# A fused decoder block on one core: setup and first two steps reordered, the second FFN matrix turned one step later, a table filled in the setup, gate sums ahead of the fourth up product

## Chip, cores, metric

One core of a Trainium2 chip runs the whole program. The metric is the device time of one execution in microseconds. The engines are TensorE (PE, matrix products), VectorE (DVE), ScalarE (ACT), GpSimd (POOL) and SyncE (SP, here the queue that issues every DMA).

## What is computed

The input x is 128 sequences of 128 tokens with 256 channels, and a context of the same shape. Three blocks with residuals follow one another:

```python
x = x + _L0_attn_ref(_layernorm(x), W_qkv, b_qkv, W_proj, b_proj)     # q k^T, a piecewise factor by bands, softmax, v, projection
x = x + _L0_xattn_ref(_layernorm(x), ctx_1024, ctx_1024, Wi_w, ...)   # 8 heads, gates and decay, normalised per head
x = x + _L0_ffn_ref(_layernorm(x), W1, b1, W2, b2, scale)             # 256 -> 1024 -> 256, gelu, a token-dependent low rank part
```

In the second block the decay between tokens i and j comes from running sums of log-sigmoid gates:

```python
itilde = einsum('bsd,hd->bhs', gate_in, Wi_w) + Wi_b
ftilde = einsum('bsd,hd->bhs', gate_in, Wf_w) + Wf_b
csum = cumsum(log_sigmoid(ftilde), axis=-1)
Dtilde = where(tril, csum_i - csum_j, -inf) + itilde_j
D = exp(Dtilde - max(Dtilde))
```

## The kernel before, in words

The 128 sequences are taken in 32 groups of four. A step `it` works on several groups at once, as a software pipeline: the first layernorm and the q and v products of group it+1 ("coming"), the self attention of group it ("own"), the gated attention of group it-1 ("cross"), and the FFN of group it-2 ("ffn"). Step 0 has the coming and own parts alone, step 1 has cross besides, and from step 2 on all four run. Steps 2 to 30 are a hardware loop, 31 to 33 are written out behind it.

There is no scheduler: each engine runs its own program in the order in which the code names the instructions, and waits on semaphore counters. What an engine waits for holds up everything behind it on that engine.

The **setup**. PE turns and multiplies the attention weights, DVE splits the results in a high and a low part, POOL writes constants. Each DVE instruction of it counts up the semaphore `s_set_v`. V_BIAS and SETUP_V are counts of it: after the biases, and after everything. `project(-1)` on PE (from L1259) makes q and v of the first group; before it PE waits for SETUP_V. POOL waits for V_BIAS, and adds the constant row `cvp` to `xb` (the residual of the attention; L610) in every step.

**W1 and W2** arrive as they lie in memory and have to be turned by PE. They are loaded into the space of `hs_all`, which the FFN first writes in step 2. `turn_w1` (L1349) writes four PSUM banks, ACT copies them to `W1h` (L746), DVE subtracts to `W1l` (L1091). `turn_w2(i)` (L1361), i from 0 to 3, writes a bank each, and ACT copies it to `W2f` (L834). In step 0, PE runs the scores (L1390), turn_w1, turn_w2(0) and (1), turns the softmax's probabilities (L1563), attends (L1574), turns xn1 (L1253), then turn_w2(2) and (3), and then `project(0)`. `turn_xn1` and the last two turns wait for ACT and for `x2` from DVE (L1147). `moving` (L1094) is a table of 32 heads by 128 columns, a sum of two small tables, which the decay products of the cross part use; DVE fills it in step 0 in two instructions. ACT's `apply_first` (L663) writes xn1, the normalised group to come.

**PE in a full step.** turn xn3 (L1253), scores (L1390), a product for the low rank part (L1409), turn xn2, then the eight up products `up(i)` (L1428) with other work between: up(0) into bank UA, `gates` (L1379), up(1) into UB, up(2) into PV, up(3) into TB, the first group of adapters `up_adapter(0)` (L1436), `sums` (L1385, L1386), up(4) into TA, `qk(0)` (L1453), up(5), up(6), qk(1), up(7), adapters again, then `decay` (L1528), `down` (L1490) and the rest. `sums` picks the gate's running sums out of `csum`. Behind it the chain on DVE is: copies of the two results to `acs` (L1042, L1043), a running maximum `acs` (L1045, semaphore acs_ok), then `em` (L1049), the split of the sums into `parts` (L1055 to L1059), and `rows` (L1063). The queue of SP copies `parts` into three rows of `moving` (L505). `qk` waits for acs_ok, since it writes the bank of `sums`:

```python
if t == 0:
    pe.wait_ge(h_ok.h, h_ok.at(it, 1))
    ...
    pe.wait_ge(acs_ok.h, acs_ok.at(it, 1))
    pe.wait_ge(gate_ok.h, gate_ok.at(it, 1))
```

`csum` itself is a scan on DVE (L1038) behind `gates`, two small DVE operations and three of ACT. POOL's order in a step is: ot (L594), vc (L600, L606), xb (L610), xg (L619, when the bands of the scores are done, y_ok), and four times Ng (L625).

Of the kernel before, what the change touches and what calls it, by code (L numbers as in the profile page):

```python
# [34 lines left out]
P = 128  # L35
D = 256
S = 128
G = 4
# [82 lines left out]
def build(nc, x, ctx_in, W_qkv, b_qkv, W_proj, b_proj, Wi_w, Wi_b, Wf_w, Wf_b, gn_w, gn_b,  # L121
# [10 lines left out]
    with ctx:  # L132
# [174 lines left out]
        RAWB = UAB + [PV, GT, DD, QQ] + UAB  # L307
# [220 lines left out]
        def _(pool):  # L528
# [60 lines left out]
            def step(it):  # L589
# [18 lines left out]
                if SELF.on(it):  # L608
                    pool.wait_ge(xb_loaded.h, xb_loaded.at(it, 16))
                    pool.tensor_tensor(xb[:, :, :], xb[:, :, :], cvp[:, :].unsqueeze(1).broadcast_to([P, G, D]),  # L610
                                       ALU.add).then_inc(xb_ok.h, 1)
# [21 lines left out]
        def _(act):  # L633
# [82 lines left out]
            def step(it):  # L716
# [25 lines left out]
                if isinstance(it, int) and it == 0:  # L742
                    for i in range(4):
                        act.wait_ge(raw_mm, i + 1)
                        hi, _ = w1_parts(i)
                        act.activation(hi, w1_turned(i), ACT.Copy).then_inc(raw_hi, 1)  # L746
                if FFN.on(it):
                    act.preload_act_table(ACT.Gelu)
# [80 lines left out]
                if coming:  # L829
                    apply_first(it)  # L830
                if isinstance(it, int) and it == 0:
                    for i in range(4):
                        act.wait_ge(raw_mm, 5 + i)
                        act.activation(W2f[:, 2 * i:2 * i + 2, :],  # L834
                                       RAWB[4 + i][:, :].rearrange("p (k o) -> p k o", k=2), ACT.Copy)\
                            .then_inc(raw_hi, 1)
# [6 lines left out]
                if cross:  # L843
                    act.wait_ge(harg_ok.h, harg_ok.at(it, 1))
                    a.link(act, act.activation(htmp[:, :], harg[:, :], ACT.Ln))
                    act.activation(hrs0[:, :], htmp[:, :], ACT.Exp, scale=-0.5).then_inc(hrs0_ok.h, 1)
                if coming:
                    evac_xn1h(it, (QQ, DD))
                    keep_v(it)
                    evac_qT(it, 0)  # L850
                if own or cross:
# [12 lines left out]
        def _(dve):  # L864
# [86 lines left out]
            dve.wait_ge(s_load, 16 * LOADS)  # L951
# [3 lines left out]
            dve.wait_ge(s_gbias, 16 * 2 * G)  # L955
            done(dve.tensor_copy(WgT[:, :, 0:16], PV[:, 0:64].rearrange("p (k n) -> p k n", k=4)))
            done(dve.tensor_tensor(sel_i[:, :], sel_i[:, :], sel_nf[:, :], ALU.add))
# [14 lines left out]
            done(dve.tensor_copy(masks[:, :, 4 * H:5 * H], both[:, :, 3 * H:4 * H]))  # L972
            done(dve.tensor_copy(rows[96:P, :, :, :].rearrange("p t f n -> p t (f n)"), masks[96:P, :, H:5 * H]))
# [694 lines left out]
```

## Time and profile before

| what | value |
|---|---|
| median of 3 runs | 1824.24 us (1824.04 to 1824.56) |
| the profiled execution, its own time | 1826.38 us |
| span of its trace | 1824.7 us |
| mean granted clock of TensorE | 0.983 of full speed |
| PE, weight loads, DVE, ACT, POOL busy | 95%, 76%, 75%, 64%, 22% |
| granted clock from 30 to 40 us, from 90 to 100 us | 0.54, 0.50 |
| PE busy in 0 to 40 us | 18.2 us |
| DMA engines busy | 19.6% |

The page lists busy time by engine, then the span in 40 slices, then the chain of work that ended last, and then groups of instructions by line. In a row such as `PE L1428 MATMUL TB<-xn3l,W1h 128*128 128x512 f32 x2`, what is written stands left of the arrow, what is read right of it, then the size of the tile of the array in rows*columns, the shape, and how many instructions the row holds. The modelled end of a matmul overlaps the start of the next; starts are what to compare. A bracket at the end tells how long the engine was idle before, and who ended it. L numbers are lines of the kernel before; those of the kernel after stand up to 19 lines lower in the file.

### The profile page before, as it was taken

What the parts mean: (1) busy time and instruction counts of PE and PEld (TensorE: products, weight loads), DVE (VectorE), ACT (ScalarE), POOL (GpSimd) and SP (SyncE); (2) the same over time, 40 slices, a digit from 0 to 9 for tenths busy, and PEclk for the clock granted to TensorE, in tenths of its full rate; (3) what the DMA queues carried; (4) which work ended last, traced back from release to release, by engine and by line L of the source; (5) the groups of instructions that cost most, each with busy time, mean ns of one, the idle gap of its engine ahead of it and who ended that gap; (6) DMA issues with size and microseconds to landing.
All of it is one profiled execution on the core that took longest, in us unless ns stands there. A gap on an engine that the chain in (4) does not pass through costs nothing.

```text
span 1824.7 us, 47628 instructions
## 1 busy us (share of the span) xinstructions
PE 1738.5 (95%) x15708; PEld 1380.1 (76%) x15708; DVE 1377.1 (75%) x4092; ACT 1172.4 (64%) x2666; POOL 395.0 (22%) x330
## 2 busy tenths in 40 slices
PE   5669999999999999999999999999999999999897
PEld 4557777788777777877777877777787777778676
DVE  4677777878777887877778777778787777877752
ACT  1457766666676666667666676766667676666552
POOL 2012222221222222122222212222212222221220
PEclk8879999999999999999999999999999999999998
DMA  5111212221121222121122112122211212221100
GB/s 140 35 38 38 61 38 61 61 60 38 47 60 39 61 61 58 32 55 50 49 61 61 55 31 60 40 59 61 60 51 34 61 38 61 61 60 38 26 16 27
DMA packets 226879, 93.05 MB, mean 51 GB/s; under 512 B 154896, under 2 KB 226320, under 8 KB 226848
## 3 DMA queue, kind: packets, MB, share of 16 engines
q1 hardware_dynamic: 226848, 92.65, 19.6%
q8 instruction: 17, 0.28, 0.1%
q14 instruction: 14, 0.11, 0.0%
HBM read 70.84 MB, written 16.78 MB: 48 GB/s over the span
## 4 chain that ended last, share of the span: by engine, by line
PE 90%; DVE 5%; issue 2%; ACT 1%; SPq 1%; DMA 0%; DVEq 0%; ACTq 0%
PE UA L1490 12%; PE TA L1490 6%; PE GT L1490 6%; PE UB L1428 5%; PE TB L1428 5%; PE PV L1428 5%; PE GT L1502 3%; PE TA L1390 3%; PE QQ L1253 3%; PE UA L1453 3%; PE UA L1428 2%; PE DD L1253 2%; PE PV L1543 2%; PE QQ L1528 2%; PE UB L1543 2%
## 5 line engine op out<-in xcount | busy, mean ns | idle before, releaser
L1124 DVE TENSOR_TENSOR C<-qT,QKs 128x512 f32<-128x512 f32 x256 | 176.7, 711 | 124.2 <-ACT qT L774 121.3
L1490 PE MATMUL UA<-W2f,hs_all 128*128 128x256 f32 x1024 | 236.3, 379 | 0.0
L1490 PEld LDWEIGHTS UA<-W2f,hs_all 128*128 128x128 f32 x1024 | 194.4, 190 | 30.4 <-issue 0.2
L594 POOL TENSOR_TENSOR ot<-xg,b_b 128x1024 f32<-128x1024 f32 x32 | 76.3, 2385 | 552.4 <-DMA out<-ot 500.2
L625 POOL TENSOR_TENSOR Ng<-HT,gnw_b 128x256 f32<-128x256 f32 x128 | 93.3, 729 | 440.1 <-DVE cden L1137 435.5
L619 POOL TENSOR_TENSOR xg<-x,gnb_b 128x1024 f32<-128x1024 f32 x32 | 75.5, 2359 | 305.4 <-DVE Evl L1116 288.2
L1490 PE MATMUL TA<-W2f,hs_all 128*128 128x256 f32 x512 | 126.0, 379 | 0.0
L1490 PE MATMUL GT<-W2f,hs_all 128*128 128x256 f32 x512 | 115.8, 379 | 0.0
L691 ACT ACTIVATE V<-QQ 128x260 f32<-128x260 f32 x32 | 12.4, 388 | 159.5 <-PE QQ L1285 159.5
L755 ACT ACTIVATE QKs<-DD 128x512 f32<-128x512 f32 x64 | 38.3, 598 | 102.3 <-PE DD L1453 102.3
L1490 PEld LDWEIGHTS GT<-W2f,hs_all 128*128 128x128 f32 x512 | 94.8, 190 | 11.7
L1490 PEld LDWEIGHTS TA<-W2f,hs_all 128*128 128x128 f32 x512 | 94.8, 190 | 11.1 <-issue 0.2
L1453 PEld LDWEIGHTS UA<-xn2T,ctxT 32*128 32x128 f32 x512 | 63.3, 190 | 40.5 <-ACT hs_all L765 25.1
L1453 PE MATMUL UA<-xn2T,ctxT 32*128 32x128 f32 x512 | 74.8, 286 | 16.0 <-DVE acs L1045 13.8
L610 POOL TENSOR_TENSOR xb<-xb,cvp 128x1024 f32<-128x1024 f32 x32 | 77.0, 2405 | 12.2 <-DVE c L950 12.2
L1253 PE MATMUL QQ<-ident,xn 128*128 128x128 f32 x380 | 63.9, 292 | 14.2 <-ACT xn L674 12.7
L774 ACT ACTIVATE qT<-DD 128x512 f32<-128x512 f32 x128 | 74.0, 578 | 2.8 <-PE DD L1528 1.5
L600 POOL TENSOR_TENSOR vc<-vc 128x992 f32<-128x992 f32 x32 | 58.9, 1842 | 77.8 <-DVE ve L888 77.8
L1453 PE MATMUL GT<-xn2T,ctxT 32*128 32x128 f32 x512 | 75.7, 288 | 0.0
L1453 PE MATMUL QQ<-xn2T,ctxT 32*128 32x128 f32 x512 | 75.6, 288 | 0.0
L1453 PE MATMUL DD<-xn2T,ctxT 32*128 32x128 f32 x512 | 75.6, 288 | 0.0
L774 ACT ACTIVATE qT<-QQ 128x512 f32<-128x512 f32 x128 | 74.8, 584 | 0.1
(392 smaller groups left out, 5350.9 us busy)
## 6 DMA issues: line engine op xcount, KB each, us to landing
xin<-x SPq DMA_DIRECT2D x32, 512.0 KB, 4.4
xb<-x SPq DMA_DIRECT2D x32, 512.0 KB, 4.1
blocks<-ctx SPq DMA_DIRECT2D x256, 64.0 KB, 2.0
vc<-ctx SPq DMA_DIRECT2D x32, 512.0 KB, 3.6
out<-ot SPq DMA_DIRECT2D x32, 512.0 KB, 3.2
Ev<-xn SPq DMA_DIRECT2D x256, 4.0 KB, 1.7
hs_all<-L_ffn_W SPq DMA_DIRECT2D x4, 512.0 KB, 8.9
E<-xn SPq DMA_DIRECT2D x128, 16.0 KB
```

The source lines that it names most:

```text
L594: pool.tensor_tensor(ot[:, :, :], x3[:, :, :], b2_b[:, :].unsqueeze(1).broadcast_to([P, G, D]), ALU.add).then_inc(xf_ok.h, 1)
L600: pool.tensor_tensor(heads[:, :, 0:HD - 1], heads[:, :, 0:HD - 1], heads[:, :, HD - 1:HD].broadcast_to([P, G * HEADS, HD - 1]), ALU.subtra ...
L610: pool.tensor_tensor(xb[:, :, :], xb[:, :, :], cvp[:, :].unsqueeze(1).broadcast_to([P, G, D]), ALU.add).then_inc(xb_ok.h, 1)
L619: pool.tensor_tensor(xg[:, :, :], x2[:, :, :], gnb_b[:, :].unsqueeze(1).broadcast_to([P, G, D]), ALU.add).then_inc(xg_ok.h, 1)
L625: pool.tensor_tensor(Ng[:, b, :].rearrange("p (k n) -> p k n", k=2), HT[:, b % 2, :, 0:P], gnw_b[:, :].rearrange("p (k n) -> p k n", k=2), ...
L774: act.activation(dx[hf], DB[hf][:, :], ACT.Exp)\
L1124: dve.tensor_tensor(C[:, b % 2, :, half], dx[hf].rearrange("p (h i) -> p h i", h=HEADS), QKs[:, b, :, half], ALU.mult)\
L1253: ins = pe.transpose(banks[c][:, b * S:(b + 1) * S], src[:, b, c * P:(c + 1) * P], ident[:, :])
L1428: pe.matmul(UP[i][:, :], w[:, k, hc * P:(hc + 1) * P], xt[:, k, :], start=(w is W1h and xt is xn3h and k == 0), stop=False)
L1453: ins = pe.matmul(QKB[r][:, (2 * b + f) * P:(2 * b + f + 1) * P], ctxT[lane, f, tok], xn2T[lane, f, tok], start=True, stop=True)
L1490: ins = pe.matmul(OB[b][:, 0:D], hs_all[:, k, b * S:(b + 1) * S], W2f[:, k, :], start=(i == 0), stop=(i == KH - 1))
L1543: ins = pe.matmul(bank[q:q + 32, (h // 4) * P:(h // 4 + 1) * P], vc[:, b, HD * h:HD * h + HD], C[:, b % 2, h, :], start=True, stop=True)
```

## The change

Nothing is computed otherwise. Eight things move:

1. PE waits before `project(-1)` for V_BIAS alone, which now includes the copy of the turned gate weights (`WgT`, L956). `turn_w1` waits for a new mark V_MASKS; the full SETUP_V is awaited ahead of turn_w2(0).
2. DVE fills `moving` at the end of the setup and no longer in step 0. Its waits for the other weights and gate biases stand behind that.
3. ACT runs `apply_first(0)` in step 0 ahead of the four copies of W1, and PE turns xn1 right behind `turn_w1`.
4. W2 is turned in step 1: (0) and (1) behind `gates`, (2) and (3) behind `sums`. ACT copies the four behind the scaled scores of step 1. With it go PE's waits for x2 and for ACT's copies in step 0.
5. In step 0, DVE computes the moments of x2 before `xn1_low`, and ACT takes the root of them before it copies v.
6. In every step with a cross part, `sums` goes ahead of up(3), so ahead of the first adapters too.
7. POOL's addition to xb waits for acs_ok in every step with a cross part, in step 0 for y_ok.
8. The banks of the turned W2 are UB, PV, TB, UB.

```diff
@@ RAWB, banks of the turned W1 and W2
-        RAWB = UAB + [PV, GT, DD, QQ] + UAB
+        RAWB = UAB + [PV, GT, UAB[1], PV, TAB[1], UAB[1]]
@@ gpsimd, step
                     pool.wait_ge(xb_loaded.h, xb_loaded.at(it, 16))
+                    if CROSS.on(it):
+                        pool.wait_ge(acs_ok.h, acs_ok.at(it, 1))
+                    else:
+                        pool.wait_ge(y_ok.h, y_ok.at(it, 1))
@@ scalar, step, behind the scaled scores
                 if isinstance(it, int) and it == 0:
+                    apply_first(it)
                     for i in range(4):
                         act.wait_ge(raw_mm, i + 1)
...
+                if isinstance(it, int) and it == 1:
+                    for i in range(4):
+                        act.wait_ge(raw_mm, 5 + i)
+                        act.activation(W2f[:, 2 * i:2 * i + 2, :],
...
@@ scalar, step, further down
-                if coming:
+                if coming and not (isinstance(it, int) and it == 0):
                     apply_first(it)
-                if isinstance(it, int) and it == 0:
-                    for i in range(4):
-                        act.wait_ge(raw_mm, 5 + i)
...
                     evac_xn1h(it, (QQ, DD))
+                if first:
+                    ln_root(1, norms_ve_ok, norms_rs0_ok, it)
+                if coming:
                     keep_v(it)
                     evac_qT(it, 0)
@@ vector, setup
-            dve.wait_ge(s_load, 16 * LOADS)
...
-            dve.wait_ge(s_gbias, 16 * 2 * G)
...
+            for t in range(2):
+                heads = slice(2 * HEADS * t, 2 * HEADS * (t + 1))
+                done(dve.tensor_tensor(moving[:, heads, :].rearrange("p h (f i) -> p h f i", f=2),
...
+            dve.wait_ge(s_load, 16 * LOADS)
+            dve.wait_ge(s_gbias, 16 * 2 * G)
@@ vector, step 0
-                    for t in range(2):
-                        heads = slice(2 * HEADS * t, 2 * HEADS * (t + 1))
-                        link(dve.tensor_tensor(moving[:, heads, :].rearrange("p h (f i) -> p h f i", f=2),
...
@@ tensor, turn_xn1, before project(-1), turn_w1
-                if isinstance(it, int) and it == 0:
-                    pe.wait_ge(raw_hi, 6)
...
-            pe.wait_ge(s_set_v, V_WT + 6)
-            pe.wait_ge(s_set_v, SETUP_V)
+            pe.wait_ge(s_set_v, V_BIAS)
             project(-1)
...
                 pe.wait_ge(s_load, 16 * LOADS)
+                pe.wait_ge(s_set_v, V_MASKS)
@@ tensor, turn_w2
-                if i >= 2:
-                    pe.wait_ge(raw_lo, i - 1)
-                    pe.wait_ge(x2_ok.h, x2_ok.at(0, G))
+                if i == 0:
+                    pe.wait_ge(v_ok.h, v_ok.at(0, G))
+                elif i == 3:
+                    pe.wait_ge(raw_hi, 5)
@@ tensor, step
                     turn_w1()
-                    turn_w2(0)
-                    turn_w2(1)
+                    turn_xn1(0, (QQ, DD))
...
                     if i == 0 and cross:
                         gates()
+                    if isinstance(it, int) and it == 1 and i == 0:
+                        pe.wait_ge(s_set_v, SETUP_V)
+                        turn_w2(0)
+                        turn_w2(1)
+                    if i == 2 and cross:
+                        sums()
                 if ffn:
                     up_adapter(0)
-                if cross:
-                    sums()
+                if isinstance(it, int) and it == 1:
+                    turn_w2(2)
+                    turn_w2(3)
...
-                if coming:
-                    turn_xn1(it, (QQ, DD))
-                if isinstance(it, int) and it == 0:
-                    turn_w2(2)
-                    turn_w2(3)
-                    pe.wait_ge(raw_hi, 8)
-                    pe.wait_ge(raw_lo, 4)
+                if isinstance(it, int) and it == 0:
+                    pe.wait_ge(raw_lo, 4)
+                elif coming:
+                    turn_xn1(it, (QQ, DD))
```

How the instructions stand, at three places. First PE in step 0, from the scores to the first product of `project(0)`. Before (L1349 is turn_w1, L1361 turn_w2, L1563 the turned probabilities, L1574 attend, L1253 turned xn1, L1273 project):

```order
L1390 MATMUL TA<-xn1T,qT 128x128 x8
...
L1349 MATMUL GT<-ident,hs_all 64x128 x8
L1361 MATMUL DD<-ident,hs_all 64x128 x8
L1361 MATMUL QQ<-ident,hs_all 64x128 x8
L1563 MATMUL TB<-ident,bands 128x128 x4
L1574 MATMUL TB<-V,sc 128x256 x2
L1574 MATMUL GT<-V,sc 128x256 x2
L1253 MATMUL QQ<-ident,xn 128x128 x4
L1253 MATMUL DD<-ident,xn 128x128 x4
L1361 MATMUL UA<-ident,hs_all 64x128 x8
L1361 MATMUL UB<-ident,hs_all 64x128 x8
L1273 MATMUL QQ<-Wvh,xn3h 128x260 x2
```

The same stretch after the change (L1403 scores, L1361 turn_w1, L1267 turned xn1, L1582, L1593, L1285 as above):

```order
L1403 MATMUL TA<-xn1T,qT 128x128 x8
...
L1361 MATMUL GT<-ident,hs_all 64x128 x8
L1267 MATMUL QQ<-ident,xn 128x128 x4
L1267 MATMUL DD<-ident,xn 128x128 x4
L1582 MATMUL TB<-ident,bands 128x128 x4
L1593 MATMUL TB<-V,sc 128x256 x2
L1593 MATMUL GT<-V,sc 128x256 x2
L1285 MATMUL QQ<-Wvh,xn3h 128x260 x2
```

Four groups of 8 have left PE's step 0, and xn1 is turned before the probabilities.

Second, ACT in step 0 and the start of its step 1, after the change (L743 scaled scores, L667 apply_first, L751 copies of W1, L806 exponentials, L812 copy of the turned probabilities, L659 and L689 copies of xn1, L643 and L644 root):

```order
L743 ACTIVATE sc<-TA,rowterm 128x128 x4
L667 ACTIVATE xn<-xin,nmr,rs 128x256 x4
L751 ACTIVATE W1h<-UA 128x2x64x4
...
L806 ACTIVATE bands,psums<-bands,nmx 128x128 x4
L812 ACTIVATE sc<-TB 128x512
L659 ACTIVATE xn1T<-QQ 128x512
L659 ACTIVATE xn1T<-DD 128x512
L689 ACTIVATE xn3h<-QQ 128x512
L689 ACTIVATE xn3h<-DD 128x512
L643 ACTIVATE lv<-ve 128x4
```

Between the copy of the probabilities and that of xn1 there was `apply_first` and the four copies of W2.

Third, PE in the loop. Before (L1428 up, L1436 adapters, L1385 and L1386 sums, L1453 qk):

```order
L1428 MATMUL PV<-xn3l,W1h 128x512 x2
L1428 MATMUL TB<-xn3h,W1h 128x512 x2
L1428 MATMUL TB<-xn3h,W1l 128x512 x2
L1428 MATMUL TB<-xn3l,W1h 128x512 x2
L1433 ISA
L1436 MATMUL UA<-T,Ef 128x512
...
L1385 MATMUL DD<-csum,sel_i 32x128
L1386 MATMUL DD<-csum,sel_f 32x128
L1421 REGISTER_ALU
L1428 MATMUL TA<-xn3h,W1h 128x512 x2
```

After (L1440 up, L1448 adapters, L1398 and L1399 sums):

```order
L1440 MATMUL PV<-xn3l,W1h 128x512 x2
L1398 MATMUL DD<-csum,sel_i 32x128
L1399 MATMUL DD<-csum,sel_f 32x128
L1440 MATMUL TB<-xn3h,W1h 128x512 x2
L1440 MATMUL TB<-xn3h,W1l 128x512 x2
L1440 MATMUL TB<-xn3l,W1h 128x512 x2
L1445 ISA
L1448 MATMUL UA<-T,Ef 128x512
...
L1433 REGISTER_ALU
L1440 MATMUL TA<-xn3h,W1h 128x512 x2
```

The two products of `sums` stand six up products and four adapters earlier. The order on SP's queue is the same as before.

## Rows read from the trace of the kernel before

**Rows 1.** The page: busy time of TensorE, and the chain that ended last by engine.
```profile
PE 1738.5 (95%) x15708; PEld 1380.1 (76%) x15708; DVE 1377.1 (75%) x4092; ACT 1172.4 (64%) x2666; POOL 395.0 (22%) x330
...
PE 90%; DVE 5%; issue 2%; ACT 1%; SPq 1%; DMA 0%; DVEq 0%; ACTq 0%
```

**Rows 2.** Who waited for whom on PE: us in total, times, longest us.
```profile
PE UA L1453 <- DVE acs L1045: 13.8, 29, 1.3
```

**Rows 3.** Timeline of PE in step 13: start us, us, what.
```profile
727.15 0.63 PE L1428 MATMUL PV<-xn3l,W1h 128*128 128x512 f32 x2
...
728.55 0.63 PE L1428 MATMUL TB<-xn3l,W1h 128*128 128x512 f32 x2
729.11 0.50 PE L1436 MATMUL UA<-T,Ef 32*128 32x512 f32 x1
...
729.55 0.30 PE L1385 MATMUL DD<-csum,sel_i 128*32 128x128 f32 x1
...
729.89 0.73 PE L1428 MATMUL TA<-xn3h,W1h 128*128 128x512 f32 x2
...
730.92 0.63 PE L1428 MATMUL TA<-xn3l,W1h 128*128 128x512 f32 x2
731.99 0.34 PE L1453 MATMUL UA<-xn2T,ctxT 32*128 32x128 f32 x1 [0.43 <-DVE acs L1045]
```

**Rows 4.** Timeline of DVE, POOL and the SP queue, same step.
```profile
727.16 0.42 DVE L1038 TENSOR_TENSOR_SCAN csum<-carry,GT 128x128 f32<-128x128 f32 x1
...
729.06 2.40 POOL L610 TENSOR_TENSOR xb<-xb,cvp 128x1024 f32<-128x1024 f32 x1
...
730.64 1.09 DVE L1045 TENSOR_TENSOR_SCAN acs<-acs 32x128 f32<-32x128 f32 x1
...
734.44 1.81 SPq L505 DMA_DIRECT2D moving<-parts  x3
```

**Rows 5.** One line, the scan of acs, all 32: duration ns min/median/max.
```profile
L1045 DVE TENSOR_TENSOR_SCAN acs<-acs x32: 411/1095/1176, 86.5 to 1746.5; 32x128 f32<-32x128 f32 x32
```

**Rows 6.** Timeline of PE, same step, second group of adapters and what follows.
```profile
738.79 0.50 PE L1436 MATMUL TA<-T,Ef 32*128 32x512 f32 x1
...
739.23 0.39 PE L1528 MATMUL DD<-moving,rows 128*128 128x512 bf16 x1
```

**Rows 7.** Timeline of the setup, DVE and then PE.
```profile
27.35 2.17 DVE L957 TENSOR_TENSOR sel_i<-sel_i,sel_nf 128x32 f32<-128x32 f32 x1
...
35.66 0.77 PE L1273 MATMUL QQ<-Wvh,xn3h 128*128 128x260 f32 x2 [9.91 <-DVE centre L980]
```

**Rows 8.** The chain that ended last, step 0: start us, us, what.
```profile
47.36 0.43 DVE bands L1074
...
55.48 2.20 DVE moving L1094
...
61.55 1.67 DVE x L1147 x4
63.36 1.99 PE UA L1361 x16
...
69.64 0.99 PE QQ L1273 x4
```

**Rows 9.** Timeline of step 0: DVE, ACT, and PE's first attend.
```profile
42.95 0.23 DVE L985 TENSOR_SCALAR rowterm<-V,c 128x4 f32<-128x4 f32 x1 [7.39 <-ACT V L691]
...
47.36 1.15 ACT L746 ACTIVATE W1h<-UA 128x512 fp32r<-128x512 f32 x1
...
50.24 1.17 ACT L746 ACTIVATE W1h<-GT 128x512 fp32r<-128x512 f32 x1
51.74 0.40 ACT L795 ACTIVATE bands<-bands,nmx 128x128 f32<-128x128 f32 x1 [0.34 <-DVE nmx L1086]
...
54.63 2.07 ACT L663 ACTIVATE xn<-xin,nmr,rs 128x256 f32<-128x256 f32 x4
...
54.79 1.13 PE L1574 MATMUL TB<-V,sc 128*128 128x256 f32 x4 [0.69 <-ACT sc L801]
```

More of the change, by code:

```diff
@@ L746, in step @@
                         act.activation(hi, w1_turned(i), ACT.Copy).then_inc(raw_hi, 1)
+                if isinstance(it, int) and it == 1:
+                    for i in range(4):
+                        act.wait_ge(raw_mm, 5 + i)
+                        act.activation(W2f[:, 2 * i:2 * i + 2, :],
+                                       RAWB[4 + i][:, :].rearrange("p (k o) -> p k o", k=2), ACT.Copy)\
+                            .then_inc(raw_hi, 1)
                 if FFN.on(it):
@@ L846, in step @@
                     act.activation(hrs0[:, :], htmp[:, :], ACT.Exp, scale=-0.5).then_inc(hrs0_ok.h, 1)
+                first = isinstance(it, int) and it == 0
                 if coming:
                     evac_xn1h(it, (QQ, DD))
+                if first:
+                    ln_root(1, norms_ve_ok, norms_rs0_ok, it)
+                if coming:
                     keep_v(it)
                     evac_qT(it, 0)
-                if own or cross:
+                if (own or cross) and not first:
                     ln_root(slice(1 if own else 2, 3 if cross else 2), norms_ve_ok, norms_rs0_ok, it)
@@ L954, in _ @@
             dve.wait_ge(s_zero, 1)
-            dve.wait_ge(s_gbias, 16 * 2 * G)
             done(dve.tensor_copy(WgT[:, :, 0:16], PV[:, 0:64].rearrange("p (k n) -> p k n", k=4)))
+            assert setup[0] == V_BIAS, setup[0]
             done(dve.tensor_tensor(sel_i[:, :], sel_i[:, :], sel_nf[:, :], ALU.add))
@@ L972, in _ @@
             done(dve.tensor_copy(masks[:, :, 4 * H:5 * H], both[:, :, 3 * H:4 * H]))
+            assert setup[0] == V_MASKS, setup[0]
             done(dve.tensor_copy(rows[96:P, :, :, :].rearrange("p t f n -> p t (f n)"), masks[96:P, :, H:5 * H]))
@@ L1209, in step @@
                         [P, G * HEADS, HD]), ALU.mult))
-                if coming:
+                if coming and cross:
                     xn1_low(it)
@@ L1222, in step @@
                     ln_moments(norms, norms_ve_ok, link)
+                if coming and not cross:
+                    xn1_low(it)
                 if own or cross:
@@ L1577, in attend @@
                         ins.then_inc(px_mm.h, 1)
+                if isinstance(it, int) and it == 1:
+                    pe.wait_ge(raw_hi, 8)
                 if cross:
@@ L1644 @@
 V_WT = 7 + 2 + 1
[L1645 to L1646 removed]
+V_BIAS = V_WT + 2 + 4 + 4 + 6 + 1
+V_MASKS = V_BIAS + 1 + 1 + 3 + 3 + 3 + 2
+SETUP_V = V_MASKS + 2 + 4 + 4 + 2
 def kernel(**inputs):
```

12 lines of the change are left out of this document (3 added, 9 removed).

## The prediction

> **What bounds the kernel now.** I read the page first. TensorE is busy 95% of the span, and the chain that ended last runs over PE for 90% of it [rows 1]. So PE's time is the kernel's time, and a change pays only where PE stands idle on the path: in the start, where PE works 18.2 us of the first 40, and in the small seams of the 31 full steps. The list of who waited for whom names the one seam that recurs: the first product of qk(0), L1453, waits 29 times for the running maximum acs on DVE, 13.8 us in all, the longest 1.3 [rows 2]. The longest is step 1; the other 28 are loop steps, 3 to 30. Then I read one loop step, instruction by instruction [rows 3, 4, 6], and the start as timeline and as chain [rows 7 to 9].
>
> In the loop step, watch the starts of PE. Matmul pairs of an up product follow each other every 0.47 us (three pairs from 727.15 to 728.55) [rows 3]. From the last pair of up(3) to the adapters it is 0.56, from adapters to `sums` 0.44, from `sums` to up(4) 0.34. From the last pair of up(4) to qk(0) it is 1.07 us, where the other passage from up to a smaller tile takes 0.56. So 0.51 us a step is real waiting. What is waited for is the scan of acs: it takes 1.09 us here and 1.095 in the median, but 0.411 at best [rows 5]. The scan began at 730.64, inside POOL's xb addition (729.06 to 731.46), and ended after it [rows 4].
>
> In the start, `project(-1)` stands 9.9 us idle for the last constant of the setup [rows 7]; in step 0 DVE fills `moving`, two instructions of about 2.2 us, between the bands and x2, and `project(0)` starts at 69.64, behind x2, two turned parts of W2 and ACT's copies [rows 8].
>
> **The loop, part by part.** *Sums ahead of up(3).* The products are the same; only seams change. Before: pair to pair 0.47, up to adapters 0.56, adapters to sums 0.44, sums to up 0.34, together 1.81 us [rows 3]. After: up to sums 0.56 (I take up to adapters for it, the nearest row), sums to up 0.34, up to adapters 0.56, adapters straight to a full-size product 0.44, which is what the second adapters show (738.79 to 739.23) [rows 6]. Together 1.90, so 0.09 us more a step.
>
> That is what changes of tile size cost here: the new order has four between up(2) and up(4), the old three. The Trainium skill, TensorEngine Tiling (Array Packing), Key Properties, speaks against the change: switching the tiling mode, not just the tile, drains TensorE. The trace agrees that each switch costs, in the starts named above. The page gives no price; the sum goes by the seams of the rows.
>
> *Is `csum` there in time?* `sums` would now start at 727.15 + 0.56 = 727.71; the scan of csum ends at 727.58 [rows 3, 4]. It fits by 0.13 us, about as long as a semaphore may need, so I charge nothing, and keep 0.3 us a step as the other end. Nothing ahead of it on its path moves.
>
> *acs.* The two copies and the scan come 1.8 us earlier. The scan then starts near 728.9 and ends at 729.3, since POOL now holds xb back until acs_ok. qk(0) comes behind up(4) at about 731.6. The wait is gone with 2 us to spare. The next in line is GELU of the first bank, since the first adapters are 0.4 us later: done at about 730.9, also in time. Gain 0.51 less 0.09, 0.42 us in 28 steps: 11.8. Steps 2, 31 and 32 only pay the 0.09. **Loop: 11.5 us less.** The ends: 14 less if the new seam costs nothing, 0 if it costs as much as the wait did.
>
> *POOL's xb behind acs_ok.* It runs from about 729.4 to 731.8. Queued behind it is only xg, which waits for the bands anyhow. What it can now hold is the DVE work behind acs: em, the split into parts. These began after 731.73 before (the scan's end) [rows 4], so even if all of it is held to 731.8 it is not later than it was. The Trainium skill, SBUF — State Buffer, Who interferes with whom, says that a DVE instruction with two SBUF inputs is blocked for the whole of a GpSimd instruction that reads SBUF. The stretched scan agrees, with 1.095 against 0.411 us [rows 5]. By that rule the parts come at the hour they came at before; by the rows I found the same, so the sum does not move. Behind the parts, the queue of SP issues their copy at 734.44, when it is through with other transfers, and the decay product comes at 739.23 [rows 4, 6]. I cost it at nothing; the cover is that queue.
>
> **The start.** *Setup.* `project(-1)` may go once the gate weights are copied, just before 27.35, instead of 35.66: 8.3 us [rows 7]. But DVE is late next. From 27.35 it still has the rest of the setup, less 2.0 us, since `sel_i` (32 columns, 2.17 us) was held by POOL's first xb, which now waits for y_ok, plus the two fills of `moving`, 4.5 us [rows 7, 8]. So DVE reaches step 0 at 35.6 - 2.0 + 4.5 = 38.1, against 42.95 for its first instruction, `rowterm` [rows 9]. PE has made v, q and the scores of group 0 by then, whatever its clock. From `rowterm` to the bands DVE and ACT took 4.4 us; now some 4.1, as the scores no longer come last. Bands at 42.2 against 47.36 [rows 8].
>
> *Step 0.* ACT takes the scaled scores until 42.2, then apply_first (2.07), then four copies of W1 (47.36 to 51.41, 4.05): it is free at 48.3 [rows 9]. The bands need 4.4 us, to 46.6, so the exponentials wait for ACT and start at 48.3 instead of 51.74. From there to the first attend took 3.05 us: 51.35. Beside it DVE does W1l until about 50.5, with nothing to fill behind. Next on ACT are the copies of xn1, four of about 0.5 us behind that of the probabilities: `project(0)` can start at 53.5. If PE's clock has fallen (PE would idle some 4 us twice ahead of it; in the slice of 30 to 40 us, with the 10 us idle of the setup, the granted clock was 0.54, so part of it at 1.2 GHz) the four attends take 3.5 us and not 1.9, and it starts at 55. Before: 69.64 [rows 8]. So 14.6 to 16.1 less; I take 15.5. The last part of project(0) wants xn1_low, now behind the moments of x2: about 58, when PE arrives near 59. Fine.
>
> *Step 1.* Four groups of W2, 16 matmuls each; one took 1.99 us behind a long wait [rows 8], about 1 at full clock. Two lie in PE's wait for csum, two in that for acs (1.3 us, rows 2). Together they fill these waits and stick out by 0.3 us; at half clock by 3. I take 0.3 more. SP, the moves of the gate weights' waits behind the fills, and the other banks cost nothing: all loads have landed by then, and every bank named is free until the next up product.
>
> **Sum:** 11.5 + 15.5 - 0.3 = 26.7 us less. Against the profiled execution's own 1826.38 that is 1799.7; the runs' median stands 2.1 lower, 1824.24, which gives **1797.5 us**.
>
> **Rivals.** (a) *The wait moves to csum.* 0.13 us of room is little; if `sums` waits 0.3 us in each step, 28 steps keep 0.12, 3.4 us instead of 11.8, and the time is 1806. For it: the narrow room. Against: in the row it fits, and nothing ahead of csum is moved. 0.15. (b) *Tile changes cost more.* The rule on draining, taken as a mechanism here: up to sums drains a full-size stream of 512 columns and the adapters straight to up(4) another. If each of the two new passages costs 0.15 more than its stand-in, 28 steps keep 0.12 again, 3.4 us of 11.8, and the time is 1806 too. The page that would have it so is the Trainium skill's TensorEngine Tiling (Array Packing), Key Properties. 0.1. (c) *The start gives less.* DVE's fill now stands before everything of step 0; if POOL's xb of step 0 (2.4 us behind y_ok) holds the W1l subtractions, or the clock is low throughout, 10 us are left of 15.5: 1803. 0.13. (d) *The end on the other side:* POOL's xb behind acs_ok holds the parts on DVE, so that their copy is issued late and decay on PE waits for it, in every loop step. It eats the gain only once parts come so late that the copy lands after 739.2. The last of three issues goes out near 735.7 and lands some 2 us later (estimate), so the queue must be held by over 1.0 us, and to end above 1828 by 2.0 (30.5 us over 31 steps and the 1.0 of room). xb would have to hold DVE for two such lengths. 0.02. (e) *More than said:* both ends best, 1791. 0.05. The forecast itself gets 0.55, its own range 1794 to 1802.
>
> **Numbers.** The range takes in (a) to (c), with both ends of start and loop in part: 1790 to 1809. Some 0.2% (3.6 us) is what a measurement of this kernel tells from no change; all but (d) and a little beyond lie below 1820. Faster 0.96, same 0.02, slower 0.02.
>
> **What would show it.** In the trace after: `project(-1)` starts near 27.5; `rowterm` of step 0 near 38; `project(0)` near 53.5 to 55; the scan of acs takes 0.41 in every step; qk(0) no longer waits for acs, and 0.56 us lie between the last pair of up(4) and it; up(2)'s last pair to sums 0.56 (if 0.8, rival a); adapters to up(4) 0.44 (if more, rival b); the period of a loop step falls by about 0.4 us. The prediction is wrong if it falls by under 0.2 us, or if `project(0)` starts later than 57.

## The result, and the profile after

| | before | after |
|---|---|---|
| median | 1824.40 us (1824.04 to 1825.13, 4 runs) | 1802.68 us (1801.92 to 1803.04, 4 runs) |
| profiled execution, own time | 1826.38 us | 1803.04 us |
| span of the trace | 1824.7 us | 1801.3 us |
| mean granted clock | 0.983 | 0.984 |

The ratio is 0.9879, 95% interval 0.9865 to 0.9894. The medians lie 21.7 us apart, the two profiled executions 23.3.

The page of after, busy times and the chain that ended last, answers to [rows 1]:

```profile
PE 1742.0 (97%) x15708; PEld 1376.2 (76%) x15708; DVE 1420.7 (79%) x4092; ACT 1172.1 (65%) x2666; POOL 402.0 (22%) x330
...
PE 94%; DVE 3%; ACT 1%; issue 1%; DMA 0%; SPq 0%; DVEq 0%; ACTq 0%
```

PE does the same instructions. Its idle time, span less busy time, falls from 86.2 to 59.3 us. The chain runs over PE for 94% of the span, not 90%. That is more than the idle time: before, the chain left PE in each loop step for 2.0 us, from the end of `sums` over DVE to qk(0) (729.99 to 731.99 in the step of [rows 3]), and now it stays on PE. DVE is busy 43.6 us longer without one instruction more; that is dealt with below.

Who waited for whom on PE, after (total us, times, longest). The row for acs [rows 2] is gone:

```profile
PE QQ L1267 <- ACT xn L678: 12.7, 3, 4.7
...
PE PV L1562 <- issue: 4.5, 1, 4.5
PE QQ L1285 <- ACT xn3h L689: 4.3, 1, 4.3
...
PE QQ L1285 <- DVE WgT L963: 1.6, 1, 1.6
```

No row has a wait left that recurs in each step: those with few counts belong to the start and to the end. `project(-1)` now waits 1.6 us for the gate weights, not 9.9 for the last constant [rows 7].

PE in a loop step of after (start us, us, what), against [rows 3]:

```profile
709.30 0.63 PE L1440 MATMUL PV<-xn3l,W1h 128*128 128x512 f32 x2
709.87 0.30 PE L1398 MATMUL DD<-csum,sel_i 128*32 128x128 f32 x1
...
710.21 0.72 PE L1440 MATMUL TB<-xn3h,W1h 128*128 128x512 f32 x2
710.77 0.63 PE L1440 MATMUL TB<-xn3h,W1l 128*128 128x512 f32 x2
...
711.80 0.50 PE L1448 MATMUL UA<-T,Ef 32*128 32x512 f32 x1
...
712.23 0.72 PE L1440 MATMUL TA<-xn3h,W1h 128*128 128x512 f32 x2
...
713.26 0.63 PE L1440 MATMUL TA<-xn3l,W1h 128*128 128x512 f32 x2
713.82 0.37 PE L1465 MATMUL UA<-xn2T,ctxT 32*128 32x128 f32 x1
```

From the last pair of up(4) to qk(0) it is 0.56 us now, where it was 1.07: nothing waits. Up to `sums` is 0.57, adapters to up(4) 0.43. But look at the pairs of up(3): from the first to the second it is 0.56, between the others 0.47. The first pair behind a change of tile size is 0.09 to 0.10 longer.

DVE and POOL in the same step, against [rows 4]:

```profile
710.95 0.41 DVE L1063 TENSOR_TENSOR_SCAN acs<-acs 32x128 f32<-32x128 f32 x1
...
711.61 2.41 DVE L1068 TENSOR_SCALAR acs<-acs 32x128 f32<-32x128 f32 x1
...
711.51 2.43 POOL L614 TENSOR_TENSOR xb<-xb,cvp 128x1024 f32<-128x1024 f32 x1
```

The scan is at its best time, 0.41 us, in every step. The 2.4 us in which POOL runs xb now fall on the small instruction that changes the sign of acs. It took 0.21 us before. Over all 32 steps it takes 75.0 us and no longer 6.6, while the scans give back 19.5 (32.7 before, 13.2 after); the two together are more than all that DVE is busy more. In the groups by line:

```profile
L1068 DVE TENSOR_SCALAR acs<-acs 32x128 f32<-32x128 f32 x32 | 75.0, 2345 | 0.0
```

The start of after, from the timelines of DVE and PE and the chain that ended last, against [rows 7 to 9]. First the timeline of DVE:

```profile
27.39 0.22 DVE L963 COPY WgT<-PV 128x64 f32<-128x64 f32 x1
27.65 0.19 DVE L965 TENSOR_TENSOR sel_i<-sel_i,sel_nf 128x32 f32<-128x32 f32 x1
33.64 4.62 DVE L993 TENSOR_TENSOR moving<-pick,masks 128x2048 bf16<-128x2048 bf16 x2
38.29 0.23 DVE L1003 TENSOR_SCALAR rowterm<-V,c 128x4 f32<-128x4 f32 x1
```

then PE's timeline at `project(0)`:

```profile
54.46 0.99 PE L1285 MATMUL QQ<-Wvh,xn3h 128*128 128x260 f32 x2
```

and the chain:

```profile
44.29 3.70 ACT W1h L751 x4
47.99 1.40 ACT bands L806 x8
...
51.24 2.07 PE TB L1593 x4
53.31 1.71 PE GT L1593 x4
55.02 0.87 PE QQ L1285 x4
...
62.67 2.02 PE TA L1403 x16
...
80.91 4.45 issue
...
106.28 1.71 PE TA L1292 x4
```

`sel_i` takes 0.19 us instead of 2.17, DVE fills `moving` in the setup and reaches `rowterm` at 38.29 (before 42.95), `project(0)` starts at 54.46 (before 69.64), the scores of step 1 at 62.67. The chain has 55.02 for `project(0)`, since it counts the attends up to their modelled end.

Where the 23.4 us of span come from can be read off the first instruction of the scores in several steps. The last column is the difference of the two kernels; what it changes by from row to row is what that stretch gave:

| scores of | before | after | difference |
|---|---|---|---|
| step 1 | 78.38 | 62.67 | -15.71 |
| step 2 | 130.09 | 115.58 | -14.51 |
| step 3 | 184.36 | 169.99 | -14.37 |
| step 31 | 1680.83 | 1656.88 | -23.95 |
| end of span | 1824.7 | 1801.3 | -23.4 |

So the start gives 15.7, steps 1 and 2 take 1.3 back, 28 loop steps give 9.6 (their period falls from 53.45 to 53.10 us), and the last steps take 0.5.

### The profile page after: what moved, and what is told of

Its sections match the earlier page's. It is cut to its first block, busy times and chain, and to the rows that moved or that the text cites. A ratio compares the mean times of both kernels' runs of the same rounds, so it can differ in the third digit from the quotient of the medians.

```text
span 1801.3 us, 47658 instructions
## 1 busy us (share of the span) xinstructions
PE 1742.0 (97%) x15708; PEld 1376.2 (76%) x15708; DVE 1420.7 (79%) x4092; ACT 1172.1 (65%) x2666; POOL 402.0 (22%) x330
## 4 chain that ended last, share of the span: by engine, by line
PE 94%; DVE 3%; ACT 1%; issue 1%; DMA 0%; SPq 0%; DVEq 0%; ACTq 0%
PE UA L1509 12%; PE TA L1509 6%; PE GT L1509 6%; PE UB L1440 6%; PE TB L1440 6%; PE PV L1440 5%; PE GT L1521 3%; PE UA L1465 3%; PE QQ L1267 3%; PE TA L1403 3%; PE TA L1440 3%; PE UA L1440 3%; PE DD L1267 2%; PE PV L1562 2%; PE UB L1562 2%; PE QQ L1547 2%
## 5 line engine op out<-in xcount | busy, mean ns | idle before, releaser
L1509 PEld LDWEIGHTS TA<-W2f,hs_all 128*128 128x128 f32 x512 | 94.8, 190 | 11.1 <-issue 0.2
L1267 PE MATMUL QQ<-ident,xn 128*128 128x128 f32 x380 | 64.0, 292 | 17.0 <-ACT xn L678 12.7
L1068 DVE TENSOR_SCALAR acs<-acs 32x128 f32<-32x128 f32 x32 | 75.0, 2345 | 0.0
```

The lines of the kernel that those rows point to most:

```text
L1068: neg = v.mark(dve.tensor_scalar(acs[:, 2, :], acs[:, 2, :], -1.0, None, ALU.mult))
L1267: ins = pe.transpose(banks[c][:, b * S:(b + 1) * S], src[:, b, c * P:(c + 1) * P], ident[:, :])
L1509: ins = pe.matmul(OB[b][:, 0:D], hs_all[:, k, b * S:(b + 1) * S], W2f[:, k, :], start=(i == 0), stop=(i == KH - 1))
```

## The experiments

Diffs are against the changed kernel, unless said otherwise. Each run stands beside the kernel before on the same chip, whose median was 1824.6 to 1825.4. All kernels compute the whole result.

**Loop alone, start alone.** The first has the setup and steps 0 and 1 of the kernel before, with `sums` ahead of up(3) and POOL's wait for acs_ok; the second has the new setup and first steps, with `sums` in its old place and no wait in steps with a cross part.

```diff
@@ loop alone, against the kernel before
                     pool.wait_ge(xb_loaded.h, xb_loaded.at(it, 16))
+                    if CROSS.on(it):
+                        pool.wait_ge(acs_ok.h, acs_ok.at(it, 1))
...
+                    if i == 2 and cross:
+                        sums()
                 if ffn:
                     up_adapter(0)
-                if cross:
-                    sums()
@@ start alone, against the changed kernel
-                    if CROSS.on(it):
-                        pool.wait_ge(acs_ok.h, acs_ok.at(it, 1))
-                    else:
+                    if not CROSS.on(it):
                         pool.wait_ge(y_ok.h, y_ok.at(it, 1))
...
-                    if i == 2 and cross:
-                        sums()
                 if ffn:
                     up_adapter(0)
+                if cross:
+                    sums()
```

> The kernel before with only the two edits that touch every step: sums ahead of up(3), and POOL's xb behind acs_ok in the steps with a cross part. Theory A (two parts that add up: the loop gives 0.34 us in each of 28 steps, about 9.7, and pays 0.2 in steps 2, 31 and 32; the start gives the rest): about 1815, 9 to 10 us under before, the period of a loop step 53.10 against 53.45. Rival B (the loop gain needs the new start, or is larger than the traces say and the start gives less): more than 2 us away from that.

> The changed kernel with sums back behind the first adapters and POOL's xb waiting for nothing in steps with a cross part (in step 0 still for y_ok). Theory A: the start alone, about 12 to 14 us under before, 1811 to 1812.5, period 53.45, qk(0) waits for acs again 28 times. Rival B: the start alone gives the 15.5 us predicted, 1809.

Loop alone: 1815.95 us, ratio 0.9954 (0.9940 to 0.9967), 8.7 less. Start alone: 1810.79, ratio 0.9922 (0.9908 to 0.9935), 13.8 less. Together 22.5, and the whole change gave 21.7 against its own runs of the kernel before: within the noise the two parts add up. In the second, qk(0) waits for acs as before:

```profile
PE UA L1463 <- DVE acs L1061: 12.1, 28, 0.5
```

**Sums early, POOL free; sums late, POOL behind acs_ok.** These take the loop's change apart.

```diff
@@ sums early, POOL free
-                    if CROSS.on(it):
-                        pool.wait_ge(acs_ok.h, acs_ok.at(it, 1))
-                    else:
+                    if not CROSS.on(it):
                         pool.wait_ge(y_ok.h, y_ok.at(it, 1))
@@ sums late, POOL behind acs_ok
-                    if i == 2 and cross:
-                        sums()
                 if ffn:
                     up_adapter(0)
+                if cross:
+                    sums()
```

> The changed kernel without POOL's wait for acs_ok. Theory A (the early sums alone do the work; the scan of acs would then end just before POOL's xb starts): same as the changed kernel within 1 us, 1802 to 1804. Rival B (xb is at work when the scan starts, the scan is stretched to 1.1 us again; but qk has 2 us of room): the time is the same too, only the scan's duration tells. Rival C (POOL's wait was what mattered): the wait of qk comes back, 1808 or more.

> The changed kernel with sums back behind the first adapters, POOL's wait for acs_ok kept. Theory A (the real wait of 0.51 us was the stretched scan; with POOL held back the scan takes 0.41, acs is ready 0.2 us before qk(0) needs it, and there is no further change of tile size): the wait goes and the 0.18 us a step for the new seams is saved, so 5 us under the changed kernel, near 1797.5, period 52.94. Rival B (0.2 us of room is too little and some wait is left): between 1798 and 1803. Rival C (sums had to be early): no better than 1809, the wait of 0.5 us is back.

Sums early without POOL's wait: 1802.65 us, ratio 0.9879 (0.9864 to 0.9894), the time of the changed kernel. The wait is worth nothing once `sums` is early. xb then holds the instruction just behind the scan (`em`, mean 2.26 us), and the scan itself in only some steps, 0.54 us in the mean; nobody is late for it.

POOL's wait with `sums` in its old place: 1831.44 us, ratio 1.0035 (1.0021 to 1.0049). That is 6.8 us slower than the kernel before by the medians, in spite of a start that gives 14 us, and it refutes my expectation. The wait of qk(0) is gone, as expected, but the period is 54.12 us. The list of who waited for whom shows a new one:

```profile
PE PV L1562 <- DVE C L1136: 35.1, 29, 1.2
```

Here are DVE, POOL and PE in one step of that kernel, by their timelines:

```profile
725.57 2.41 DVE L1068 TENSOR_SCALAR acs<-acs 32x128 f32<-32x128 f32 x1
...
737.90 2.50 DVE L1136 TENSOR_TENSOR C<-qT,QKs 128x512 f32<-128x512 f32 x2
...
725.47 2.42 POOL L614 TENSOR_TENSOR xb<-xb,cvp 128x1024 f32<-128x1024 f32 x1 [2.08 <-DVE acs L1063]
736.85 2.41 POOL L623 TENSOR_TENSOR xg<-x,gnb_b 128x1024 f32<-128x1024 f32 x1 [8.95 <-DVE Evl L1128]
...
725.76 0.37 PE L1465 MATMUL UA<-xn2T,ctxT 32*128 32x128 f32 x1
...
740.45 0.65 PE L1562 MATMUL PV<-C,vc 128*32 128x128 f32 x16 [1.21 <-DVE C L1136]
```

and the same in the kernel before, where qk(0) starts at 731.99 [rows 3]:

```profile
744.15 1.29 DVE L1124 TENSOR_TENSOR C<-qT,QKs 128x512 f32<-128x512 f32 x2 [2.10 <-ACT qT L774]
...
741.09 2.36 POOL L619 TENSOR_TENSOR xg<-x,gnb_b 128x1024 f32<-128x1024 f32 x1 [9.62 <-DVE Evl L1116]
```

Count from qk(0). C starts 12.1 us behind it in both kernels, because it waits for ACT's copy of the decay products. But xg, which POOL may begin once DVE is through with the bands, starts 9.1 us behind qk(0) before and 11.1 here: DVE's chain is held 2.2 us instead of 0.68, and qk(0) comes 0.5 earlier. Before, xg is over at 11.5 and C runs free in 1.29 us. Here xg reaches to 13.5, C takes 2.50, and the product that reads C comes 1.21 us late. Per step: 53.45 less the 0.51 of the old wait plus 1.21 is 54.15, against 54.12 measured. In the kernel before, POOL's xb (729.06 to 731.46) lies for its first 0.95 us beside DVE's wait for `sums`, then beside the two copies out of PSUM, which keep their 0.28 us, and holds only the scan, for 0.68 us. In the changed kernel the scan starts 2.87 us ahead of qk(0) (710.95 against 713.82), not 0.85 as here (724.91 against 725.76), and DVE can afford the hold: xg starts 9.08 us behind qk(0) (722.90 against 713.82) and C is free:

```profile
725.96 1.29 DVE L1136 TENSOR_TENSOR C<-qT,QKs 128x512 f32<-128x512 f32 x2 [2.10 <-ACT qT L785]
...
722.90 2.35 POOL L623 TENSOR_TENSOR xg<-x,gnb_b 128x1024 f32<-128x1024 f32 x1 [8.96 <-DVE Evl L1128]
```

**xb behind the parts, with early and with late sums.** Is it the held instruction that matters, or that DVE is held at all?

```diff
                     if CROSS.on(it):
-                        pool.wait_ge(acs_ok.h, acs_ok.at(it, 1))
+                        pool.wait_ge(parts_ok.h, parts_ok.at(it, 1))
```

> The changed kernel with POOL's xb behind parts_ok. Theory A: nothing on PE's path in the loop (no wait there to remove), so the period stays 53.10; in step 1, where decay waits for the copy of the parts, these come 2.1 us sooner: 1 to 2 us under the changed kernel, 1801. Rival B: xb behind parts holds the bands and pv waits: over 1804.

> The kernel of e4_pool_only (sums behind the first adapters), with POOL's xb behind parts_ok instead of acs_ok. In e4 xb started right behind the scan and held the next DVE instruction, a tensor_scalar with one input in SBUF, for 2.41 us; bands, xg and the first products C came late, and pv waited 1.2 us a step. Theory A (it is xb's hold on the DVE chain behind acs that cost 29 us): with xb behind the parts the scan is short and the chain is not held either, the wait of qk for acs goes, and no seam is added: about 1798, 4 to 5 us under the changed kernel. Rival B (xb now holds the bands, two tensor_scalars, and pv waits again): over 1805.

With early sums 1802.55 us, ratio 0.9879 (0.9863 to 0.9894); with late ones 1830.83, ratio 1.0029 (1.0019 to 1.0040). In both xb now holds `rows`; with late sums:

```profile
726.12 3.02 DVE L1081 SCALAR_TENSOR_TENSOR rows<-parts,own_row,masks 96x256 bf16<-96x256 bf16 x2
...
736.41 2.48 DVE L1136 TENSOR_TENSOR C<-qT,QKs 128x512 f32<-128x512 f32 x2
...
PE PV L1562 <- DVE C L1136: 34.7, 29, 1.2
```

Both miss what was expected of them. With early sums the 1 to 2 us of step 1 didn't come, and with late ones the hold had only moved to `rows`. Whether the sign change is held or `rows` makes no difference to the time. What counts is that DVE stands over 2 us behind a late `sums`, and that this moves xg onto C (735.33, again 11.1 us behind qk(0)). Early sums are the part that pays.

**One more change of tile size.** Two tiny products (128x32, in the tile of `sums`) between up(1) and up(2), in all steps with cross and ffn; nothing uses their result.

```diff
+                    if i == 1 and cross and ffn:
+                        pe.matmul(DD[32:64, 0:P // 4], sel_i[:, :], sel_i[:, :], start=True, stop=True)
+                        pe.matmul(DD[0:32, 0:P // 4], sel_f[:, :], sel_i[:, :], start=True, stop=True)
                     if i == 2 and cross:
```

> The changed kernel with two small products (constants, 128 rows by 32 columns of the array, result not used) between up(1) and up(2) in every step with cross and FFN parts, 31 of them. Theory A (what sums costs ahead of up(3) is the seam: up to sums 0.56, sums to up 0.34, a first pair that is 0.10 longer, less the 0.47 of a plain pair; 0.1 less since the products have a quarter of the columns): 0.4 to 0.5 us a step, 13 to 16 us slower than the changed kernel, 1816 to 1819. Rival B (a change of tile size costs next to nothing, and the 0.17 us a step by which the loop gave less than predicted is something else): under 1807.

1813.04 us, ratio 0.9935 (0.9921 to 0.9949): 10.4 us more than the changed kernel. The period rises from 53.10 to 53.50. PE in one step:

```profile
712.48 0.63 PE L1440 MATMUL UB<-xn3l,W1h 128*128 128x512 f32 x2
713.04 0.22 PE L1481 MATMUL DD<-sel_i 128*32 128x32 f32 x1
...
713.23 0.72 PE L1440 MATMUL PV<-xn3h,W1h 128*128 128x512 f32 x2
713.79 0.62 PE L1440 MATMUL PV<-xn3h,W1l 128*128 128x512 f32 x2
```

From the last pair of up(1) to the second pair of up(2) it is 1.31 us, where two plain pairs take 0.94. So a passage to small tiles and back costs 0.37 us. The products themselves are a small part of it: from a small product to the next full one it is 0.19 us with 32 columns and 0.34 with the 128 of `sums`, so by an estimate from these two the 32 columns take some 0.05. The run lies below the 13 to 16 us expected, which had put the seams at 0.4 to 0.5 us. The Trainium skill, TensorEngine Tiling (Array Packing), Key Properties, says that a switch of the tiling mode drains TensorE. This run agrees that a switch costs, and gives the price here, 0.37 us; it doesn't show the draining itself.

**Where the start's gain is.** Two kernels against each other: the fill of `moving` back in step 0, behind W1l; and the same with `project(-1)` behind the whole setup again.

```diff
@@ fill in step 0
-            for t in range(2):
-                heads = slice(2 * HEADS * t, 2 * HEADS * (t + 1))
-                done(dve.tensor_tensor(moving[:, heads, :].rearrange("p h (f i) -> p h f i", f=2),
...
                         dve.tensor_tensor(lo, w1_turned(i), hi.bitcast(F32), ALU.subtract).then_inc(raw_lo, 1)
+                    for t in range(2):
+                        heads = slice(2 * HEADS * t, 2 * HEADS * (t + 1))
+                        link(dve.tensor_tensor(moving[:, heads, :].rearrange("p h (f i) -> p h f i", f=2),
@@ all of the setup awaited (besides)
             pe.wait_ge(s_set_v, V_BIAS)
+            pe.wait_ge(s_set_v, SETUP_V)
             project(-1)
```

> The changed kernel with the two fills of moving back in step 0, behind the W1l subtractions. Theory A: DVE reaches rowterm 4.6 us sooner, the exponentials come 4.6 sooner, but the fill then stands between W1l and x2 (adds of x2 would wait until about 50.5 - 4.6 + 4.6 = 50.5 and more, about when attend is done), so project(0) starts about as early or 2 to 4 us earlier: 1799 to 1803. Rival B (the fill in the setup was what gave the gain of the start): 4 us slower than the changed kernel, 1807.

> The kernel of e7_fill_in_step0 with PE waiting for the whole setup ahead of project(-1), as the kernel before does. Theory A (with the fill out of the way, DVE reaches step 0 at 33.6 and would wait for v of group 0, which now comes 6 to 7 us later): 1804 to 1807. Rival B (DVE's chain hides project(-1) anyhow): same as e7, 1799.

Fill in step 0: 1799.22 us, ratio 0.9868 (0.9852 to 0.9884), by the medians 3.5 us **less** than the changed kernel. But only three of its four executions took 1799.1 to 1799.2, at a mean clock of 0.988; the fourth took 1804.6 at 0.985, more than any of the changed kernel. In the trace, of a quick one, DVE reaches the bands earlier (37.40 against 42.25), the exponentials start at 42.80 and `project(0)` at 49.03, 5.4 us earlier. The fill (45.42 to 50.04) then lies beside PE's attends and holds up x2 behind it: in `project(0)` PE waits 1.2 us for x2 and 2.2 for `xn1_low`, and the scores of step 1 start at 59.98, 2.7 us earlier. From the scores of step 0 to those of step 1 the two kernels compare as follows, the changed kernel first (us, then PE, weight loads, DVE, ACT and POOL busy, granted clock, DMA share, GB/s):

```profile
34.60:62.67 28.07, 19.59 (x136) 16.66 (x137) 24.41 (x66) 13.97 (x35) 2.38 (x1) 0.76 0.25 57
...
34.17:59.98 25.81, 17.59 (x137) 14.81 (x137) 24.23 (x63) 13.94 (x35) 2.39 (x1) 0.93 0.27 62
```

PE idles 8.5 us in the first and 8.2 in the second. The other 2.0 us are PE's own busy time for the same products, at 0.93 of the clock and not 0.76. So most of this gain shows as clock and not as less waiting, and in one execution of four it didn't come.

All of the setup awaited: 1810.13, ratio 0.9917 (0.9903 to 0.9931), 10.9 us more than the median with the fill in step 0 and above the 1804 to 1807 expected. In PE's timeline `project(-1)` starts 6.5 us later (33.77 against 27.24) and its pairs take 0.43 us, not 0.24:

```profile
33.77 0.77 PE L1285 MATMUL QQ<-Wvh,xn3h 128*128 128x260 f32 x2 [7.64 <-DVE centre L989]
34.34 0.64 PE L1285 MATMUL QQ<-Wvl,xn3h 128*128 128x260 f32 x2
```

The scores of step 0 come 9.3 us later (43.44 against 34.17). So most of the start's gain is this one wait: 10.9 us, where loop and start of the kernel with the fill in step 0 gave 26.2 together and the loop alone 8.7. And the idle time costs more than its length, since PE comes out of it at a lower clock: 0.50 granted in 30 to 40 us, against 1.00 in the same ten with the fill in step 0, and `project(-1)` takes 8.05 us from its first pair to its last, not 5.32.

**Where step 1 loses.** The last two turned parts of W2 go behind the third decay product of step 1, ACT's copies with them.

```diff
@@ tensor, step 1
-                if isinstance(it, int) and it == 1:
-                    turn_w2(2)
-                    turn_w2(3)
...
                     decay(1, 0)
+                    if isinstance(it, int) and it == 1:
+                        turn_w2(2)
+                        turn_w2(3)
                     pv(0)
```

> The changed kernel with the last two turned parts of W2 in step 1 moved behind decay(1,0), where PE idles 4.5 us ahead of pv(0), ACT's two copies with them. Theory A (PE's low clock in step 1, 0.50 from 80 to 90 us, is what made step 1 1.7 us longer): the work in the idle keeps or brings back the clock, and step 1 loses 1 to 2 us: 1801. Rival B (the clock falls as before and the two parts only stand in another place): same within 1 us.

1799.36 us, ratio 0.9858 (0.9843 to 0.9873), 3.3 us less than the changed kernel; all four executions lie within 1799.0 and 1799.9. The wait that the profile puts down to "issue" ahead of pv(0) is 0.99 us, not 4.5. From 80 to 90 us, with the same columns as above, the changed kernel:

```profile
80.00:90.00 10.00, 5.29 (x45) 3.45 (x44) 7.14 (x16) 4.96 (x16) 2.44 (x2) 0.50 0.00 1
```

and with W2 late:

```profile
80.00:90.00 10.00, 8.51 (x83) 6.28 (x83) 8.03 (x17) 7.13 (x21) 3.11 (x2) 0.79 0.01 2
```

The two parts now lie where PE would idle, and PE works at 0.79 there rather than 0.50. From the scores of step 1 to those of step 2 it takes 50.6 us, not 52.9. Is that the clock, as was expected, or the filled wait? The same table for the whole of step 1 tells; the rows are the changed kernel, W2 late, and the run with sums early and POOL free, which has the turned parts where the changed kernel has them:

```profile
62.67:115.58 52.91, 33.98 (x341) 27.03 (x342) 37.67 (x105) 29.70 (x74) 9.75 (x8) 0.80 0.07 21
...
62.77:113.35 50.58, 33.85 (x341) 27.14 (x342) 37.67 (x105) 29.28 (x74) 9.77 (x8) 0.85 0.07 23
...
63.68:115.23 51.55, 32.55 (x341) 26.10 (x342) 37.42 (x104) 29.67 (x74) 9.85 (x8) 0.84 0.07 22
```

With W2 late PE is busy as long as in the changed kernel and idles 16.7 us, not 18.9. So 2.2 of the 2.3 us are the filled wait, and not the clock. The third row shows what the clock does: the same 19.0 us idle, but 1.4 us less busy time for the same products, at 0.84 granted and not 0.80.

**Both, and xb early in step 0.** The fill in step 0 together with W2 late; and the changed kernel without the new wait for y_ok or acs_ok.

```diff
@@ xb early
                     if CROSS.on(it):
                         pool.wait_ge(acs_ok.h, acs_ok.at(it, 1))
-                    else:
-                        pool.wait_ge(y_ok.h, y_ok.at(it, 1))
```

> The changed kernel with both edits of e7_fill_in_step0 and e9_w2_late. Each alone gave 3.3 us. Theory A (one saves in step 0, the other in step 1, and they add): 1796. Rival B (both end on the same later wait or the same clock phase): 1799.

> The changed kernel without POOL's wait for y_ok in step 0, so its first xb runs in the setup as before. Theory A (it holds sel_i on DVE for 2.17 us, and DVE is the late one in the start): 2 us slower than the changed kernel, 1804.7. Rival B (the hold is hidden): 1802.7.

Both together: 1801.54 us, ratio 0.9877 (0.9861 to 0.9893). Of its four executions two took 1798.8 and 1799.0 at a mean clock of 0.989, two 1804.1 and 1804.4 at 0.984. None comes near the 1796 of two gains that add, and the quick ones lie within 0.3 us of the quickest of either edit alone. Why a kernel with the fill in step 0 has these two times, no run shows. xb early in step 0: 1803.61, ratio 0.9885 (0.9869 to 0.9901), 0.9 us more than the changed kernel and within the interval, so between the two theories it decides nothing. The scores of step 1 start 1.7 us later, and the end is 0.5 later.

The fastest version is thus the changed kernel with two parts of W2 turned later (1799.4). With the fill left in step 0 and `project(-1)` behind V_BIAS alone, five of the eight executions of the two runs are as fast (1798.8 to 1799.2), and the other three took 1804.1 to 1804.6.

## Why the prediction was right, and where it missed

1797.5 us was forecast and 1802.7 measured, inside the range of 1790 to 1809, but 0.7 us above the forecast's own 1794 to 1802. It lies next to the 1803 of rival (c), though not by its mechanism, for the start gave what was forecast. 26.7 us of gain were forecast against the profiled execution, 23.3 came by its own time. The remaining 1.8 us lie in the reference: the profiled execution of before stood 2.1 us above the median, that of after only 0.4.

- *The start, 15.5.* Right: 15.7 by the scores of step 1. `project(-1)` at 27.67 (27.5 forecast), `rowterm` at 38.29 (38.1), exponentials at 47.73 (48.3), `project(0)` at 54.46 (53.5 to 55; the attends ran slowly, the case named for the upper end). That `sel_i` was held by POOL came true as well. Not seen: that the fill of `moving` in the setup is no gain. Left in step 0 it gave 1799.2 in three executions of four.
- *qk(0)'s wait, 0.51 a step.* Right in size and cause: it is gone, and the scan takes 0.41 us.
- *The seams of `sums`, 0.09 a step.* This is the term that was mis-sized: 0.18. I counted the four passages, but not that the first pair behind each change of tile takes 0.10 more (710.21 to 710.77 against 0.47); up(3) had no such change ahead of it before. 0.51 less 0.18 is 0.33, and the period fell by 0.34 to 0.35. Over the loop that is 9.6 us instead of 11.8, and the last steps cost 0.5 and not 0.2. It is rival (b) in kind, at 0.09 instead of its 0.3.
- *csum in time.* Right: up to sums is 0.57 us in the loop. Rival (a) fell; only step 1 waits, 0.2 us.
- *POOL's xb at nothing.* Right, and by the first reason given: DVE's chain starts 1.8 us earlier, so that even when it is held until POOL is through, the parts come no later than before. They end at the same place counted from qk(0) (715.80 against 713.82, before 733.99 against 731.99). The cover named at the end, the queue of SP, wasn't needed. What the prediction didn't see is what the same hold does without the head start. The runs with late sums show it: DVE's chain then stands 2.0 us later against qk(0), xg falls on C, and the product pv waits 1.2 us a step. Rival (d), slower than before, is real there, at 5.4 and 6.8 us; its victim is pv and not decay.
- *The port rule.* I used the rule of two SBUF inputs for the scan and took `em` and the split for what could be held. The changed kernel shows L1068, an instruction with one SBUF input, held for 2.41 us. The Trainium skill, SBUF — State Buffer, Who interferes with whom, says that `tensor_scalar` can enter a mode that uses both ports and then contends too; the trace agrees that it is held, with 2.41 against 0.21 us, but doesn't show the mode.
- *Step 1, 0.3.* In the traces steps 1 and 2 took 1.3 us more (107.3 against 106.0). The turned parts do lie in the two waits that I put them into: the 2.3 us for `csum` and the 1.3 for acs are gone but for 0.2. But PE idles 4.5 us ahead of pv(0), where it idled 3.8, and `project(1)`'s products of 106.28 took 1.71 us, where the same four took 1.00 before. The clock is low in both kernels (0.50 from 80 to 90 us here, 0.50 from 90 to 100 before), and it shifts such a sum by itself: with the turned parts in the same place, the two steps took 105.2 us in the run with sums early and POOL free, and 108.2 with xb behind the parts and early sums. So whether the parts stick out by 0.3 or by 1.3 stays open. What the run with W2 late does show is that I chose the wrong wait: behind decay they fill the long one, and that is worth 3.3 us.

## What to carry over

When one engine's long instruction can hold another's short ones, don't ask only which of them it stretches: follow the held chain to the next long instruction of the first engine, and see what that one falls on. A chain that starts earlier can absorb the hold; the same wait without that head start cost more than it freed. Price a moved small-tile product by all its seams, the first full-size pair behind it included, and put filler work into the longest wait of the bounding engine (here 4.5 us ahead of pv(0)), not into the first one that it fits.

## What the hardware showed that I had not expected

- A 32x128 `TENSOR_SCALAR` on DVE with one SBUF input took 2.41 us instead of 0.21 while POOL ran an addition of two SBUF operands that started 0.10 us before it. In other steps and runs DVE was held in the same way in the scan (1.09), `em` (2.50), `rows` (3.02 for two) and C (2.50 for two). Copies out of PSUM beside the same addition kept their 0.28 us.
- The first pair of 128x512 products behind a change of tile size took 0.56 us to the next, others 0.47; a passage to a small tile and back 0.37 us in all.
- For the same products of step 1 PE was busy 33.98 us at a granted clock of 0.80 and 32.55 us at 0.84, in two kernels that differ in one wait of POOL.
